# A three-layer graph network with an expert layer behind it: own products of the layers' last tiles put off, and the last phase reordered

## The reference, cut to what matters

```python
h = layernorm(x)
for l in range(3):
    h_neigh = segment_sum(h[src], dst) / max(deg, 1)
    rst = relu(h @ W_self[l] + h_neigh @ W_neigh[l] + b[l])
    h = rst / max(norm(rst), 1e-12)
x = x + h
xn = layer_norm(layernorm(x), ln_g, ln_b)
logits = xn @ Wg                        # 8 experts, the best two are used
o = gelu(xn @ W1 + b1) @ W2 + b2        # per expert, hidden size 64
x = x + layer_norm(layernorm(x) + combined(o, logits), out_g, out_b)
```

## Time and profile before

| what | value |
|---|---|
| median of 3 runs | 2169.52 us (2165.85 to 2169.86) |
| the profiled execution's own time | 2180.63 us |
| its span | 2178.5 us |
| mean granted clock of TensorE | 0.97 |
| PE, PEld | 2035.9 us (93%), 1139.4 us (52%) |
| DVE | 1722.8 us (79%) |
| ACT | 995.7 us (46%) |
| POOL | 1264.7 us (58%) |
| phase 0, until the first aggregation | 516.0 us |
| phase 1, from its first aggregation to that of phase 2 | 496.3 us |
| phase 2, to the first aggregation of the last phase | 496.6 us |
| last phase, from there to the end | 669.6 us |

### The profile page before, as it was taken

One profiled execution on the slowest core, in us unless ns is written; L12 is line 12 of the kernel. 1 busy time (PEld: TensorE's weight loads), 2 busy tenths in 40 slices (PEclk: granted clock), 3 DMA queues, 4 the chain that ended last, 5 costly groups with the idle time before them and its releaser, 6 DMA issues.

```text
span 2178.5 us, 43921 instructions
## 1 busy us (share of the span) xinstructions
PE 2035.9 (93%) x15309; PEld 1139.4 (52%) x15315; DVE 1722.8 (79%) x4122; ACT 995.7 (46%) x1699; POOL 1264.7 (58%) x1396
## 2 busy tenths in 40 slices
PE   6999899997999999997999999996399999999997
PEld 3444444443444444443444444442177777777775
DVE  7678986555888888885888888885589999999984
ACT  4454333332333333332333333333576676666641
POOL 2784116674666666653444444444578888888854
PEclk9999999998999999998999999998599999999998
DMA  6764339973555555553666666664678888888853
GB/s 205 165 166 133 122 136 138 120 118 114 174 174 174 174 174 174 174 169 132 217 217 217 217 217 218 217 218 163 165 154 173 172 178 180 175 172 174 179 85 43
DMA packets 246208, 364.11 MB, mean 167 GB/s; under 512 B 115577, under 2 KB 115751, under 8 KB 245991
## 3 DMA queue, kind: packets, MB, share of 16 engines
q1 hardware_dynamic: 185175, 195.88, 35.4%
q0 software_dynamic: 60816, 165.43, 28.9%
HBM read 175.81 MB, written 165.31 MB: 157 GB/s over the span
## 4 chain that ended last, share of the span: by engine, by line
PE 74%; DVE 7%; POOL 7%; issue 5%; ACT 3%; DMA 3%; SPq 0%; DVEq 0%; POOLq 0%; ACTq 0%
PE psS L494 29%; PE psY L494 23%; PE psY L1736 10%; PE psT L1660 4%; POOL slot_table L655 3%; PE psA L1704 2%; PE psA L1705 2%; POOL node_info L655 2%; PE psS L1760 1%; DMA slot_table<-area 1%; DVE R L1370 1%; DVE area L1414 1%; PE psY L1738 1%; PE psA L1770 1%; POOL scl L676 1%
## 5 line engine op out<-in xcount | busy, mean ns | idle before, releaser
L494 PE MATMUL psY<-w_n,HT 128*128 128x512 f16 x2844 | 662.8, 383 | 22.0 <-ACT HT L877 19.9
L494 PE MATMUL psS<-w_s,HT 128*128 128x512 f16 x2844 | 652.5, 379 | 0.0
L494 PEld LDWEIGHTS psY<-w_n,HT 128*128 128x128 f16 x2844 | 279.0, 99 | 368.8 <-ACT HT L877 27.6
L494 PEld LDWEIGHTS psS<-w_s,HT 128*128 128x128 f16 x2844 | 268.5, 98 | 280.3
L904 ACT ACTIVATE RR<-R 128x512 f32<-128x512 f32 x237 | 149.5, 631 | 362.4 <-DVE R L1370 362.4
L763 POOL DMA_INDIRECT y_rows<-YB,poutT x158 | 160.9, 1018 | 188.7 <-DVE YB L1252 160.5
L756 POOL TENSOR_TENSOR scl<-ssm,halfpow 128x1 f32<-128x1 f32 x158 | 88.8, 562 | 247.0 <-DVE ssm L1388 247.0
L1262 DVE SCALAR_TENSOR_TENSOR SB<-psS,downs,bias 128x512 f32<-128x512 f32 x237 | 177.7, 750 | 55.8 <-PE psS L494 51.7
L494 PE MATMUL psS<-w_w,raw 128*128 128x512 f16 x948 | 217.4, 379 | 0.0
L1252 DVE SCALAR_TENSOR_TENSOR YB<-psY,YB 128x512 f16<-128x512 f32 x237 | 162.4, 685 | 29.4 <-ACT YB L871 29.2
L912 ACT ACTIVATE HH<-RR,scl 128x512 f16<-128x512 f32 x158 | 114.0, 722 | 149.0 <-POOL scl L756 149.0
(11 more groups left out here) (280 smaller groups left out, 3612.6 us busy)
## 6 DMA issues: line engine op xcount, KB each, us to landing
self_rows<-SB SPq DMA_DIRECT2D x236, 256.0 KB, 2.0
Sl<-self_rows SPq DMA_DIRECT2D x158, 256.0 KB, 4.0
area<-in_x_dram SPq DMA_DIRECT2D x78, 256.0 KB
y_rows<-YB SPq DMA_DIRECT2D x78, 256.0 KB, 5.1
out_dram<-obb SPq DMA_DIRECT2D x78, 256.0 KB, 4.2
raw<-in_L_gnn_W_neigh_dram SPq DMA_DIRECT2D x12, 256.0 KB
raw<-in_L_gnn_W_self_dram SPq DMA_DIRECT2D x12, 256.0 KB, 4.2
y_rows<-YB,poutT POOLq DMA_INDIRECT x158, 3.1
```

Source lines behind the costliest of these rows:

```text
L494: mm = eng.matmul(acc, lhs[:, a, c, :], w[:, bpart, c, :], start=(n == 0), stop=(stop and n == 3 * KC - 1))
```

## The change

Phases 1 and 2 leave out the own products of their last 5 and 10 tiles (`LATE`). The turned rows of these tiles are kept in buffers of their own (`HT_LATE`, `HT_LAST`), copied by ACT (`turn_late`) and not by DVE, and for them PE's transposes stand ahead of the neighbour product. The own products run in the next phase. In phase 2, four of phase 1's stand in front of step -3 and the fifth in front of step -1. In the last phase, three of phase 2's stand in front of everything and the other seven follow the aggregations of steps -4 to 2 (`own_last`). DVE's evictions and SP's stores follow suit, and each load of S waits for its own store.

In the last phase two banks take the sums in turn (`psA3`: `psA[0]` and `psT[0]`), so that the carry goes as in phases 1 and 2: `carry_lo` on DVE; `carry_rest`, `carry_rest_in` and `minus` are gone. The statistics of x2 change: x2 also sums its rows (`accum_out`), DVE makes the negative mean, and ACT squares the deviations with a sum (`x2_deviations`), in place of bn_stats and bn_aggr. `up` and `gelu` move from offset -7 to -3 with a ring of eight GEL buffers, and the lists are reordered. In phase 1, POOL no longer waits for the stores of S before its first gather, but before its first by_node, which comes one step later.

```diff
+LATE = (0, 5, 10)
+LATE_AHEAD = 3
+GEL_RING = 8
...
+def late_place(t, l):
+    k = t.t - (T - LATE[l])
+    return k if k >= 0 else None
+def late_tile(k, l):
+    return Tile(T - LATE[l] + k, max(l - 1, 0))
...
+        GEL += [sq[:, i, :] for i in range(4)] + [rawf[:, D * i:D * (i + 1)] for i in (6, 7)]
+        def turned_rows(t, l):
+            k = late_place(t, l)
+            if k is None:
+                return HT[t.slot(2)][:, :, :, :]
+            return HT_LAST[k] if l == 2 else HT_LATE[k]
+        psA3 = [psA[0][:, :], psT[0].rearrange("p a c n -> p (a c n)").bitcast(F32)]
...
# SP, phases 2 and 3
-                if l == 2:
-                    for i in range(2):
-                        sp.wait_ge(q.s2[i], 16 * ((T + 1 - i) // 2))
                 def load_self(t, s=s, l=l):
-                    after(sp, s.r, (t + -1).n)
+                    after(sp, s.r, t.n if t.t == 0 else (t + -1).n)
+                    sp.wait_ge(s.s2[t.slot(2)], Tile(t.t, l - 2).landed(2))
...
-                    run_tiles(T, [(0, store_self), (5, load_self), (2, out_bias)], 1)
+                    run_plan(T, [(0, store_early), (5, load_self), (2, out_bias)],
+                             [(-3, store_late, late_tile(k, 1)) for k in range(LATE[1] - 1)]
+                             + [(0, store_late, late_tile(LATE[1] - 1, 1))], run=1)
...
-            run_tiles(T, [(6, load_self3), (-1, turn_x)], 2)
+            run_plan(T, [(6, load_self3), (-1, turn_x)],
+                     [(max(k - LATE_AHEAD, -1) - 3, store_last, late_tile(k, 2)) for k in range(LATE[2])], run=2)
# POOL
-                    if l == 1:
-                        pool.wait_ge(last.s2[i], 16 * ((tiles + 1 - i) // 2))
...
                     if l == 1:
+                        if t.t == 0:
+                            for k in range(2):
+                                pool.wait_ge(ph[0].s2[k], 16 * ((TN + 1 - k) // 2))
                         after(pool, s.r, (t + -1).n)
...
-                        st.append((5, by_node))
+                        def by_node_late(t, by_node=by_node):
+                            if t.t == 1:
+                                by_node(Tile(0))
+                            if t.t >= 1:
+                                by_node(t)
+                        st.append((5, by_node_late))
# ACT
+            def turn_late(t, l):
+                if late_place(t, l) is None:
+                    return
+                s = ph[l]
+                act.wait_ge(s.tr, (t + 1).n)
+                act.activation(turned_rows(t, l), psT[t.slot(2)][:, :, :, :], ACT.Copy).then_inc(s.ht, 1)
-                run_tiles(T, [(2, hhi), (0, yhi),
+                run_tiles(T, [(2, hhi), (1, turn_late), (0, yhi),
                                       (3, carry_hi), (3, relu)], l - 1)
...
+            def x2_deviations(t):
+                t = t.own
+                i, j = t.group % 2, t.place
+                act.wait_ge(f3.mean, (t + 1).n)
+                after(act, f3.lnv, t.group - 1)
+                act.activation(bmat.rearrange("p c n -> p (c n)"), X2[t.slot(X2_RING)], ACT.Square, bias=nmean[:, i, j:j + 1],
+                               accum_out=ssx[:, i, j:j + 1]).then_inc(f3.dev, 1)
...
-            run_tiles(T, [(4, carry_hi), (-8, fhi), (4, relu), (4, sum_squares3), (4, carry_rest_in),
-                          (-7, weights_in), (-1, xn), (-1, xhi), (-3, gate_tanh), (-7, gelu)], 2)
+            run_tiles(T, [(4, carry_hi), (-8, fhi), (4, relu), (4, sum_squares3), (-7, weights_in),
+                          (3, x2_deviations), (-1, xn), (-1, xhi), (-3, gate_tanh), (-3, gelu)], 2)
# DVE, phases 1 and 2
+                late_steps = [(-3 if l == 1 or k < LATE[1] - 1 else 0, sev_late, k) for k in range(LATE[l - 1])]
# DVE, last phase
-            run_tiles(T, [(-8, hs), (3, x2), (2, group_scales), (-4, confidences), (3, x2_stats),
-                          (4, combine), (-3, logits), (-8, flo), (-3, largest), (3, x2_mean_var),
-                          (-3, largest_index), (6, one_hot), (-3, gaps), (3, group_vars),
-                          (-9, z_stats), (-3, hots), (-9, z_mean_var), (-10, result), (-9, z_gain), (-1, xlo)], 2)
+            run_plan(T, [(-8, hs), (-4, confidences), (4, carry_lo), (4, combine), (3, x2), (3, x2_mean),
+                          (-3, logits), (-8, flo), (2, group_scales), (-3, largest), (6, one_hot),
+                          (-3, largest_index), (-3, gaps), (3, group_vars), (-9, z_stats), (-3, hots),
+                          (-9, z_mean_var), (-10, result), (-9, z_gain), (-1, xlo)],
+                     [(max(k - LATE_AHEAD, -1) - 3, sev_last, k) for k in range(LATE[2])], run=2)
# PE, phases 1 and 2
-                run_tiles(T, [(0, neigh), (1, turn), (0, own), (3, aggregate)], l - 1)
+                late_steps = [(-3 if l == 1 or k < LATE[1] - 1 else -1, own_late, k) for k in range(LATE[l - 1])]
+                run_plan(T, [(1, turn_late), (0, neigh), (1, turn_early), (0, own), (3, aggregate)],
+                         late_steps, run=l - 1)
# PE, last phase
-            run_tiles(T, [(4, aggregate), (-9, down), (4, carry_rest), (-7, turn_w),
-                          (-7, up), (-7, spread_w), (-2, gate)], 2)
+            def own_last(t):
+                k = t.t + LATE_AHEAD
+                if k < LATE[2]:
+                    own_late(k, 2)
+            for k in range(LATE_AHEAD):
+                own_late(k, 2)
+            run_tiles(T, [(4, aggregate), (4, own_last), (-9, down), (-7, turn_w), (-3, up), (-2, gate), (-7, spread_w)], 2)
```

185 lines of the change are left out of this document (103 added, 82 removed).

## The result

The kernel after takes 2153.16 us in the median of 8 runs (2150.82 to 2161.62), the kernel before 2167.4 us in the same rounds: a ratio of **0.9936, interval 0.9923 to 0.9948**, 0.64% or some 14 us faster. The forecast was 32.6 us. The profiled execution took 2152.15 us, with a span of 2150.1 at a mean clock of 0.985.

A forecast was written before the change was run, and what follows sets the result against it. It took PE as the last phase's limit, DVE close behind. Terms 1.3 - 4.4 - 1.5 - 5.4 - 5.2 - 9.3 - 8.1 = -32.6 us, off the 2169.52 us median, gave 2137 us; range 2121 to 2156.

The forecast's parts named there:

- POOL becomes the limit at 29.62: Last phase, 65 steady steps: POOL's unchanged work sets 29.62 us per group of four tiles, against 30.19 before; -9.3 us.
- POOL stretches more: Rival, steady steps: scatters meet DVE at its worst, period 30.6, 6.5 us lost, total 2153 us; chance 0.15.
- DVE's floor stays 29.2: Last phase, steady steps: DVE's removed and added operations come out even, so it still needs 29.2 us a group.
- The rival that DVE sets 29.16: Rival, steady steps: DVE is the limit, not POOL; the steady part gives 16.7 us, total 2130 us; chance 0.17.
- PE's floor of 28.8: Last phase, steady steps: without the `minus` product PE needs 29.70 - 0.86, about 28.8 us a group.
- The end: Last phase, steps 82 to 85 without `up`: 4.4 us a step against 6.43, four steps by 2.0, -8.1 us.
- The opening of the last phase: First aggregation to first full step: 72.7 us against 77.9, -5.2 us, at PE's high clock, with put-off products delaying nothing.
- Ends and seams of phases 1 and 2: Ends -4.4 and -5.4 us, with ACT's loop at 5.85 us a step; seam between them -1.5; phase 1's opening +1.3.
- -4.0 us for the three steps behind the last aggregation: Ends of phases 1 and 2: put-off own products shorten the stretch after the last aggregation, -4.0 us in each phase.
- 10.8 us for the seam into the last phase: End of phase 2's last neighbour product to the last phase's first aggregation: still 10.8 us, as before.
- by_node's 1.3 us: Opening of phase 1: POOL's third gather precedes the first by_node, so tile 0's load of Sl starts later, +1.3 us.
- slower case: Rival, last phase: PE idles a little and its clock falls to 0.50; sixteen such steps give 2241 us; chance 0.05.

The follow-up runs named there:

- e7: Kernel before with GpSimd's floor under the sum of squares taken out of the last phase: 2177.02 us, 1.0018 of before.
- e2: Kernel after without GpSimd's floor under the sum of squares in the last phase, which ScalarE's squares carry as a bias: 2140.82 us, 0.9855 of before.
- e5: Kernel after with four last-phase VectorE operations (x2, xlo, flo, result) reading their second operand from PSUM, not SBUF; computation incomplete: 2134.51 us, 0.9823 of before.
- e11: Kernel after without GpSimd's floor under the sum of squares and with its addition zv made by ScalarE: 2142.48 us, 0.9856 of before.
- e13: Kernel after with only the two low parts (xlo, flo) on VectorE reading their second operand from PSUM: 2140.86 us, 0.9819 of before.
- e14: Kernel after with only x2 and the result on VectorE reading their second operand from PSUM: 2136.47 us, 0.9801 of before.
- e10: Kernel after with VectorE's last-phase order put back as in the kernel before: 2181.69 us, 1.0030 of before.
- e3: Kernel after with the last phase's DMA transposes and the waits on them left out: 2154.56 us, 0.9918 of before.

## Why the prediction was right or wrong

**The steady part was wrong, and with it half of the gain.** The step that failed is "**POOL becomes the limit at 29.62**". The first half of it is shown: e7 (POOL not the limit before), e2 and e5 (the limit after). The number is not: I took the period less POOL's waits as a fixed need, though I had seen a row of stretched scatters and knew the stretch to depend on what stands beside it. It went to 30.56, and PE, freed to 28.8, was given nothing. 15.5 of the 17.3 us by which the profiles miss the forecast stand there (13.7 to 19.4 with the other two profiles of after). The rival "POOL stretches more" gave a period of 30.6, +6.5 us and 2153; measured were 30.56, +6.2 and 2153.16 (that the total agrees to the last figure is luck, since the other terms missed by 1.8 us and the median of before moved by 2.1). Its mechanism is shown as well, with one correction: I had put the stretch on the scatter alone, which got no longer (1908 to 1899 ns). It fell on the small operations (+380 ns), of which zr had shown 566 to 570 ns at every instance. The scatter was long before already (e5 has it at 1677), so what my row told of was a stretch that the 29.62 held; what it could not hold was the one that the new order adds. 0.15 was too low for it: the change reorders VectorE's whole last phase, so the old overlap was the one thing that could not be carried over.

**"DVE's floor stays 29.2"** is neither shown nor contradicted. The fastest run with VectorE's work as in after, e11, has a group at 29.3 us. e13 and e14 went below 29.2, at 29.0 and 28.9, but with operands of VectorE changed. The rival that DVE sets 29.16 would have needed a GpSimd without stretches; e5 shows what that is worth, 29.2 us a group. **PE's floor of 28.8** holds: e14 has PE busy 399 of 400 us at 28.9.

**The end** was forecast at -8.1 and came at -8.3; 4.4 us a step against 4.07 to 4.21.

**The opening of the last phase**: 72.7 forecast, 71.2 measured. The high clock was right but not whole (0.93), and PE had one wait of 7.4 us for turned rows in it. The number came out by terms that offset each other: that the late products "delay nothing" there was wrong by 3.2 us, and the gain came with VectorE's new order (e10) and not with the clock.

**Ends and seams of phases 1 and 2**: forecast -10.0 together, -7.4 as the mean of three profiles of after against the one of before. The steps with late products were forecast at 5.85 us, set by ScalarE, and that mechanism is borne out: from 1431.73 on PE's transposes follow each other by 5.70 us, six of the eight after a wait of 1.7 to 2.6 us for ACT's HH. The aggregations run ahead of them at first, so the seven steps from 1425.93 to 1463.23 take 37.3 us for the 42.4 of before, more than forecast. **What failed is the -4.0 us for the three steps behind the last aggregation.** ScalarE's pace goes on to the last tile, whose transposes wait 2.56 us more, and from the last aggregation to the end of the last neighbour product (1463.23 to 1478.94) it is 15.7 us, where it was 14.3 before and should have been 10.3. In six such ends of three profiles of after it is 15.7 or 15.8 four times, 14.1 and 12.4:

```profile
1425.93 0.38 PE L1780 MATMUL psA<-area,Sm 128*128 128x512 f16 x1
...
1438.10 4.19 PE L523 MATMUL psY<-w_n,w_s 128*128 128x512 f16 x12
...
1463.23 0.38 PE L1780 MATMUL psA<-area,Sm 128*128 128x512 f16 x1
...
1471.64 0.97 PE L1726 MATMUL psT<-iden,HH 128*128 128x128 f16 x8 [2.56 <-ACT HH L961]
1472.40 6.70 PE L523 MATMUL psY<-w_n,raw 128*128 128x512 f16 x24
```

Twelve matmuls take 4.19 us there at 1438.10, for the usual 2.75. The window over them has PE busy throughout at a mean granted clock of 0.65, part of it at the low level (0.50), after a wait of 2.06 us for ACT's HH:

```profile
1438.00:1442.30 4.30, 4.30 (x16) 1.76 (x15) 3.02 (x8) 1.82 (x4) 2.22 (x3) 0.65 0.49 111
```

The product at 1455.18 repeats it (4.18 us), and the last two products take 6.70 us together. The forecast had no term for this. I predicted 10.8 us for the seam into the last phase; the span from the end of the last neighbour product (1478.94) to 1489.34 is 10.4. by_node's 1.3 us were not tried on their own; they are below what phase 1's spread of 493.2 to 494.7 us can show.

**No slower case came**: the clock in the steady window is 0.99, with PE 95% busy.

## What to carry to other kernels

An engine's need read off a profile (period less its waits) holds only as long as its neighbours keep their places. Where a change reorders another engine, compare the same instruction's shortest and mean times first, and price the limit from both. Before working on the longest wait in the list, ask which engine waits for nobody: here PE's waits for DMA transposes looked like the cause and were worth nothing, and one 0.3 us operation on GpSimd was worth 18 us. The version to keep is e2, which beats both kernels: 0.9855 of before.

## What the runs showed of the hardware that I had not expected

- GpSimd's root of one element a partition takes 566 to 570 ns in every instance of the kernel before, and up to 1093 ns when it starts while VectorE's 0.68 us subtraction with two SBUF operands runs: it then ends 423 to 428 ns after VectorE's operation does. With one of VectorE's operands from PSUM it is back at 566 to 570 (55 instances in e5). A VectorE operation that begins some 350 ns after the root's start left it alone in the kernel before (27 instances) and not in e3 (12 instances of 1510 to 1522 ns), which nothing here explains. Indirect DMA issues wait in the same way (scatter 1677 to 1968 ns on average).
- Such waits count as busy time. In e2 GpSimd lost an operation of 0.32 us from each step and was busy longer in 400 us (351 for 347), because the steps came faster and the rest of its operations got longer: 6.47 us a step for 6.62. So its busy share says little of what it needs.
- PE lost clock after stalls in an otherwise busy stretch. In these neighbouring windows of the kernel after, the first has PE stalled for turned rows (4.17 us, until 1759.05) and the second the lower clock behind it:

```profile
1720.00:1760.00 40.00, 34.06 (x450) 26.15 (x449) 34.77 (x100) 26.39 (x56) 34.79 (x41) 0.98 0.99 168
1760.00:1800.00 40.00, 40.00 (x468) 28.25 (x467) 37.24 (x107) 27.68 (x57) 33.38 (x37) 0.93 0.81 178
```
